# Layer-0 attention scores over the 32 rows of their head, and their pieces by pairs of heads

## What is computed

```python
h = _rms(x, n1_w)
q = _rms(heads(wq), qn_w); k = _rms(heads(wk), kn_w); v = heads(wv)
scores = jnp.einsum('bhqd,bhkd->bhqk', q, k) * HD ** (-0.5)
scores = jnp.where(causal[None, None], scores, -jnp.inf)
attn = jax.nn.softmax(scores, axis=-1)
ao = jnp.einsum('bhqk,bhkd->bhqd', attn, v)...  @ wo.T
...
moe = wts[:, 0:1] * o0 + wts[:, 1:2] * o1 + wts[:, 2:3] * o2 + wts[:, 3:4] * o3
```

## Time and profile before

| | us |
|---|---|
| median of 3 runs (1509.48 to 1510.54) | 1509.85 |
| the profiled execution | 1509.77 |
| its span, first to last instruction | 1508.0 |
| PE busy | 1393.1 (92%) |
| PE weight loads busy | 1064.7 (71%) |
| DVE busy | 1102.0 (73%) |
| ACT busy | 785.7 (52%) |
| POOL busy | 240.3 (16%) |

### The profile page before, as it was taken

How to read it: one execution, slowest core, us unless ns; L and a number is a source line. 1 busy time by engine, 2 the same in 40 slices (tenths; PEclk the granted TensorE clock), 3 DMA queues, 4 the chain that set the end, 5 groups by cost and what they waited for, 6 DMA issues and landing times.

```text
span 1508.0 us, 27908 instructions
## 1 busy us (share of the span) xinstructions
PE 1393.1 (92%) x9460; PEld 1064.7 (71%) x9460; DVE 1102.0 (73%) x3389; ACT 785.7 (52%) x1701; POOL 240.3 (16%) x355
## 2 busy tenths in 40 slices
PE   3279999999999999889948999999999999989998
PEld 2157777777777777656536777778778777768887
DVE  3688888989898887462237877888787877855555
ACT  2325465555546454443326666766766766632322
POOL 4000000000000000000042333332222332400000
PEclk9689999999999999989989999999999999999999
DMA  2000000000000000210000000000000000000000
GB/s 96 0 1 1 1 1 1 1 2 1 1 1 2 1 1 1 88 53 0 0 14 1 2 1 2 1 1 1 2 2 2 1 1 2 1 1 1 0 0 28
DMA packets 5612, 12.03 MB, mean 8 GB/s; under 512 B 112, under 2 KB 5232, under 8 KB 5232
## 3 DMA queue, kind: packets, MB, share of 16 engines
q1 hardware_dynamic: 5488, 10.44, 1.9%
HBM read 9.39 MB, written 1.05 MB: 7 GB/s over the span
## 4 chain that ended last, share of the span: by engine, by line
PE 57%; DVE 4%; POOL 1%; ACT 1%; issue 1%; DVEq 0%; ACTq 0%; POOLq 0%
PE PS L2017 9%; PE PS L2031 8%; PE PS L2085 6%; PE PS L2010 5%; PE PS L1958 5%; PE PS L2009 4%; PE PS L2098 4%; PE PS L2044 4%; PE PS L2051 4%; PE PS L1978 2%; PE PS L2059 2%; PE PS L1653 2%; PE PS L1858 1%; PE PS L1876 1%; PE PS L1933 1%
## 5 line engine op out<-in xcount | busy, mean ns | idle before, releaser
L961 ACT ACTIVATE pe_<-PS 128x512 f32<-128x512 f32 (+3 forms) x384 | 177.7, 488 | 160.0 <-PE PS L1861 119.1
L1028 ACT ACTIVATE PN<-PS,NM 128x128 f32<-128x128 f32 (+7 forms) x256 | 189.5, 742 | 105.4 <-DVE NM L1526 51.0
L1526 DVE CUSTOM_DVE_ANT_0 PS<-PS,mask_row 128x128 f32<-128x128 f32 (+7 forms) x256 | 192.4, 772 | 41.1 <-PE PS L2010 37.2
L2009 PE MATMUL PS<-KA,QA 128*128 128x512 f32 (+3 forms) x384 | 161.0, 419 | 15.2 <-DVE KA L1565 14.3
L2017 PE MATMUL PS<-ident,PN 128*128 128x128 f32 x1152 | 170.5, 275 | 1.7 <-ACT PN L1028 1.5
L1838 PE MATMUL PS<-kta,qta 128*128 128x512 f32 (+3 forms) x384 | 147.0, 416 | 6.0 <-DVE NMH L1340 2.3
L2017 PEld LDWEIGHTS PS<-ident,PN 128*128 128x128 f32 x1152 | 131.6, 141 | 27.9 <-issue 17.8
L1858 PE MATMUL PS<-qtb,kta 128*128 128x512 f32 (+3 forms) x384 | 138.9, 389 | 0.9 <-ACT pe_ L961 0.9
L2010 PE MATMUL PS<-KB,QA 128*128 128x512 f32 (+3 forms) x384 | 128.6, 347 | 0.0
L1337 DVE CUSTOM_DVE_ANT_0 PS<-PS,W 128x128 f32<-128x128 f32 (+3 forms) x256 | 124.6, 496 | 3.0 <-PE PS L1838 1.6
L2009 PEld LDWEIGHTS PS<-KA,QA 128*128 128x128 f32 x384 | 73.3, 191 | 33.5 <-DVE QA L1562 14.5
(11 more groups left out here) (260 smaller groups left out, 3112.6 us busy)
## 6 DMA issues: line engine op xcount, KB each, us to landing
W<-w SPq DMA_DIRECT2D x1, 5124.0 KB, 15.7
W<-w SPq DMA_DIRECT2D x1, 2508.0 KB, 10.8
X<-x SPq DMA_DIRECT2D x2, 512.0 KB, 4.8
out<-X SPq DMA_DIRECT2D x1, 1024.0 KB, 5.1
WOZ<-w SPq DMA_DIRECT2D x2, 256.0 KB, 4.2
```

Source lines behind the costliest of these rows:

```text
L961: act.activation(pe_[:, h, n % 2, 0:w], PS[:, 4 + h % 2, 0:w], ACT.Exp, scale=HD0 ** -0.5)\
L1028: act.activation(prob_rows(u, r), scores_of(u), ACT.Exp, bias=NM[:, u:u + 1], scale=-1.0, accum_out=SM[:, r % 2, u:u + 1]).then_inc(score_ ...
L1526: dve.tensor_tensor_reduce(scores_of(u), scores_of(u), mask_row[:, S - w:S], -HD1 ** -0.5, -MASKED, ALU.add, ALU.min, NM[:, u:u + 1]).then ...
L2009: pe.matmul(piece, query, KA[:, b, h, lo:lo + n], start=True, stop=False)
```

## The change

`PIECES0` runs over pairs of heads: for each half and pair, over the blocks and key parts, and innermost over the two heads, so that pieces 2m and 2m + 1 are of the same block and part and of two neighbouring heads. Both score products take partitions 32h to 32h + 31 of both operands instead of all 128; the rest of those partitions in the queries' copies are zeros, and what is computed stays the same. The strings, the waits, the banks and everything else stay.

```diff
-        PIECES0 = [(c, h, i, k) for c in range(2) for h in range(HG) for i in range(4 * c, 4 * c + 4)
-                   for k in range(c + 1)]
+        PIECES0 = [(c, h, i, k) for c in range(2) for two in range(0, HG, 2) for i in range(4 * c, 4 * c + 4)
+                   for k in range(c + 1) for h in (two, two + 1)]
...
-                        ins = pe.matmul(PS[:, bank, 0:w], qta[:, h, i * P:(i + 1) * P],
-                                        kta[:, b, 512 * k:512 * k + w], start=True, stop=True)
+                        rows = slice(32 * h, 32 * h + 32)
+                        ins = pe.matmul(PS[:, bank, 0:w], qta[rows, h, i * P:(i + 1) * P],
+                                        kta[rows, b, 512 * k:512 * k + w], start=True, stop=True)
...
-                        ins = pe.matmul(PS[:, 4 + h % 2, 0:w], kta[:, 1 - b, j * P:(j + 1) * P], qtb[:, h, q0:q0 + w],
-                                        start=True, stop=True)
+                        rows = slice(32 * h, 32 * h + 32)
+                        ins = pe.matmul(PS[:, 4 + h % 2, 0:w], kta[rows, 1 - b, j * P:(j + 1) * P],
+                                        qtb[rows, h, q0:q0 + w], start=True, stop=True)
```

## The result

| | before | changed |
|---|---|---|
| median | 1509.81 us (4 runs) | 1609.61 us (1592.62 to 1614.96, 4 runs) |
| ratio | | 1.0631 [1.0604, 1.0657] |
| profiled execution | 1509.77 us | 1614.52 us |
| its span | 1508.0 us | 1612.8 us |
| mean granted clock | 0.971 | 0.939 |

The account below looks back on a forecast made before the run. TensorE's own order was taken to set the 67.2 us period in layer 0's attention. Periods 72, head 1 and tail 6 us sum to 79 us on 1509.77, giving 1589 us; range 1505 to 1640.

Parts of the forecast that it names:

- The rival without a drain: Quarters of rows need no drain, so only overlap counts: 1486 us, or 1475 if all pairs overlap; chance 0.16.
- the wash: Drain without open load (9.5 us a period) is taken back by overlap and waits: about 1510 us; chance 0.04.
- the drain alone: Slower, but by the drain without the open load: 2.4 us a period, 1530 us in all; chance 0.13.
- The period: Each of seven SLOT periods in layer 0's attention grows by 10.3 us, 72 us in all.
- Changes: 105 more shape changes a period, paying drain and uncovered weight load: 17.4 us (bounds 0 and 22).
- Overlap: 32 neighbouring score products of different heads a period run side by side: 3.1 us gained (bounds 0 and 4.7).
- Waits given back: TensorE coming later absorbs 4 of its 7.1 us of waits for VectorE or ScalarE a period.
- Order of the pieces: Pieces going by pairs of heads cost 0 us, covered by VectorE's idle 8 us a period.
- The head: Before the first period: 20 shape changes in, 20 out, less overlap of 28 pairs; 1 us (from -2 to 6).
- the tail: After the periods: shape changes cost 11 us, less 0.7 for overlap and some 4 for waits; 6 us.
- a falling clock among the rivals: Granted clock goes to 1.2 GHz in parts of the stage: 1700 us or more; chance 0.03.

Follow-up runs that it names:

- e7: Changed kernel with both score products over 64 rows (those of two heads) instead of 32; median 1607.42 us, 1.0659 of the kernel before.
- e3: Changed kernel with 32 rows only in the seven SLOT periods, all 128 rows in head and tail; median 1570.02 us, 1.0383 of the kernel before.
- e4: Changed kernel with 32 rows only in head and tail, 128 rows in the SLOT periods; median 1552.07 us, 1.0273 of the kernel before.
- e8: Changed kernel plus 24 x 6 unused full-shape bf16 products in the head and as many in the tail; median 1602.06 us, 1.0599 of the kernel before.
- e2: Changed kernel with the pieces back in their old order, both score products over 32 rows; median 1629.36 us, 1.0761 of the kernel before.
- e9: Changed kernel, SLOT regrouped (two pieces, two scores, both masks), 128 rows in head and tail; 1630.26 us; its control, same order with all 128 rows, 1597.50 us.

## Why the prediction was right, and where it was off

**Direction and mechanism of the periods: right.** The array changes shape 130 times a period instead of 24 (129 by the prediction's count), and what that costs at the value products it costs at quarters of rows too. The start of a score behind training moved by 0.16 us, the piece's load starts with the piece, and the mask is later by 0.13. The rival without a drain is out; so are the wash and the drain alone (2.4 us a period), since the periods' 8 us are paid at full clock. What the Trainium skill says of draining ("TensorEngine Tiling (Array Packing)", section "Key Properties") agrees with the rows for quarters of rows as well: a score behind training starts 0.205 us after it, where a training pass of 128 columns gives way after 0.11.

**The period: 8.1 us against 10.3 forecast, by terms that erred both ways.**
- Changes: 15.6 us against 17.4. The 0.20 and 0.21 for training to score and back were 0.16 each; to the mask 0.13 instead of 0.10; from the mask 0.11 instead of 0.15.
- Overlap: 6.9 us against 3.1, above my upper bound of 4.7. I counted the shorter stream of each pair of different heads and took two thirds. 27 of the 32 pairs start within 0.02 us of each other, the other five 0.11 to 0.37 us apart. The sum left out a second gain: with full shape the second product's load is partly open (0.32 us from a 512-column product to the next score, where 512 columns at 0.12 us for 256 are 0.24), and side by side it runs beside the first's. That is the likely reason why a neighbour gains 0.19 us and not 0.15.
- Waits given back: 1.8 us against 4. The sum of TensorE's waits rose from 7.1 to 8.9 us. I had the training chain's waits shrink since its products come later; the largest of them in sum (for `sl`, L1239) grew from 2.2 to 3.0 us. The likely reason, not tested by itself, is that work put ahead of a chain delays the chain's own products as well.
- Order of the pieces: 0.8 us a period where I said 0.

**The head: 21.8 us against 1, the tail: 23.7 against 6.** This is the step that failed. Both were costed by changes of shape at the clock of before. The tail's shape term was fair (8 us by e7 against 6); the other 15, and at least 9 of the head's, are the granted clock. I had a falling clock among the rivals, with 0.03, and placed it in the periods, arguing from the value products, narrow too, which run at 1.00. They are a small part of a period. In head and tail, with less other work between the narrow products, the clock came up later or fell (e3, e4), and filling the tail with full-shape work kept it up (e8). The periods weren't safe either: e2 and e9 lost clock in them.

**The total** of 99.8 us against 79 is nearer than its terms, and that is luck: the periods' 15 us too many stand against the ends' 38 too few. It lies in the range since that reached up to 1640 us, for waits and overlaps that gave nothing back; no part of it was meant for head and tail at the lower clock.

## What to carry to other kernels

A product over 32 rows isn't shorter than one over 128; it is only cheaper beside others of other quarters, and here each change between shapes took back 0.1 to 0.16 us, so that by these prices it takes runs of three or more narrow products, with everything they need ready at once, before it pays. That is an estimate: no kernel here came out faster by it. e9, with such runs, was only 0.4 us a period ahead of its control where its clock was full, and far behind in all. Count the changes of shape along the engine's real order of instructions, masks and transposes included, before narrowing a product. And look at the granted clock of stages in which narrow products dominate: in the tail here it cost some 15 us, the changes 8.

## What the runs showed of the hardware

- Changing between 128*128 and 32*128 costs TensorE about what changing to 128*32 does (0.09 to 0.10 us at the value products): training to a score 0.205 us from start to start, where a 128-column pass gives way after 0.11. Loads aren't fetched across a change: in the changed kernel's periods every score's load behind a product of another shape starts within 0.002 us of its product. With 128 rows it starts up to 0.03 us ahead behind training, and up to 0.24 us ahead behind another score.
- Four score products (fp32r, a rounded fp32) of 512 columns in four quarters of rows, to four banks, take 0.43 us from the first start to the next product of another shape (e9), two take the same (changed kernel, 339.80 to 340.23), and the loads of those two run side by side.
- At nearly the same busy share the granted clock differed: in the tail 66.87 of 67.3 us busy came with 0.72 with 32 rows (57.78 of 58.2 with 0.85 in another execution of the same instructions), 51.99 of 52.4 with 1.00 with 64 rows, and 59.68 of 59.7 with 1.00 with 32 rows and full-shape products added between. In the head 64 rows came with 0.63, as 32 did in e4.
